# Four graph layers on one core: message sums of the first layer into fixed PSUM regions, PE's targets loaded once a slot

## The reference

```python
# layer 0 (the one that the change is in)
msg  = relu(x[src] + edge_attr @ We + be)
aggr = segment_sum(msg, dst, num_segments=N)
h    = x + aggr
h    = relu(h @ W1 + b1) @ W2 + b2            # then batch norm and relu
# layer 1: two graph convolutions with weights d(u)^-1/2 d(v)^-1/2
# layer 2: two relation layers
agg   = segment_sum(transformed[etype, src] * (1 / in_degree[dst]), dst)
h_new = agg + h @ loop_w[l] + bias[l]
# layer 3: ten steps  out = spmm(out) * 0.9 + h * 0.1
```

## Time and profile before

| | us |
|---|---|
| median of 3 runs | 9681.38 |
| lowest, highest | 9676.89, 9699.11 |
| the profiled execution, its own time | 9793.55 |
| its span, first to last instruction | 9791.8 |

### The profile page before, as it was taken

One profiled execution on the slowest core, in us unless ns is written; L12 is line 12 of the kernel. 1 busy time (PEld: TensorE's weight loads), 2 busy tenths in 40 slices (PEclk: granted clock), 3 DMA queues, 4 the chain that ended last, 5 costly groups with the idle time before them and its releaser, 6 DMA issues.

```text
span 9791.8 us, 148708 instructions
## 1 busy us (share of the span) xinstructions
PE 5881.1 (60%) x46808; PEld 4498.4 (46%) x46879; DVE 2645.2 (27%) x5985; ACT 1603.6 (16%) x3420; POOL 3344.2 (34%) x3295
## 2 busy tenths in 40 slices
PE   4444433576766666788533333532323499999998
PEld 3222221222222222288332323332323399999998
DVE  4000000344444444322422222322222411111112
ACT  1111111011233344200211111111111000000000
POOL 1444455433333333100166566266565300000000
PEclk7555555555555555599756656755655599999999
DMA  5111113411222222144222222422222366666665
GB/s 219 41 41 40 38 44 56 50 42 48 53 53 58 58 62 62 18 161 161 92 63 64 55 63 57 112 56 58 59 63 56 79 198 199 198 199 199 198 200 168
DMA packets 531551, 915.44 MB, mean 93 GB/s; under 512 B 223435, under 2 KB 365788, under 8 KB 530220
## 3 DMA queue, kind: packets, MB, share of 16 engines
q1 hardware_dynamic: 285688, 621.27, 20.7%
q0 software_dynamic: 104896, 162.89, 8.2%
q10 hardware_dynamic: 140646, 128.06, 4.2%
HBM read 705.38 MB, written 205.67 MB: 93 GB/s over the span
## 4 chain that ended last, share of the span: by engine, by line
PE 51%; issue 19%; another core or an unknown queue 18%; DVE 6%; ACT 3%; DMA 2%; DVEq 1%; ACTq 1%; POOL 0%; SPq 0%; POOLq 0%
PE bank L1311 24%; PE bank L1194 9%; PE bank L1178 5%; PE bank L1265 4%; PE bank L1047 2%; DMA relation_table<-staged_records 1%; PE bank L1336 1%; PE bank L1329 1%; DVE edge_sums L1723 1%; PE bank L1109 1%; PE bank L1112 1%; ACT staged_records L808 1%; PE bank L1097 1%; DVE onehot L1642 1%
## 5 line engine op out<-in xcount | busy, mean ns | idle before, releaser
L709 POOL DMA_INDIRECT rows<-relation_table,staged_rows x1664 | 1687.6, 1014 | 2035.1 <-DMA staged_rows<-table_rows_of_tiles 1545.1
L1194 PE MATMUL bank<-staged_records 128*128 128x448 f16 x2304 | 1066.3, 566 | 634.8 <-issue 588.3
L1311 PE MATMUL bank<-own_term,h_transposed 128*128 128x192 f16 x16464 | 1378.3, 247 | 105.7 <-DVE own_term L1838 98.0
L1311 PEld LDWEIGHTS bank<-own_term,h_transposed 128*128 128x128 fp8e4 x16464 | 1364.9, 98 | 107.2 <-issue 106.4
L709 POOL DMA_INDIRECT rows<-node_table,records_in x832 | 897.2, 1078 | 1411.3 <-DMA records_in<-rec_dst 1128.5
L694 POOL DMA_INDIRECT rec_dst<-staged_records,staged_record_rows x781 | 753.3, 965 | 919.0 <-ACT staged_record_rows L817 536.3
L1311 PE MATMUL bank<-own_term,staged_records 128*128 128x192 f16 x12348 | 1032.4, 246 | 0.0
L1311 PEld LDWEIGHTS bank<-own_term,staged_records 128*128 128x128 fp8e4 x12348 | 1020.0, 98 | 0.0
L1723 DVE TENSOR_TENSOR edge_sums<-edge_sums,bank 128x96 f32 x1664 | 421.3, 253 | 1989.8 <-PE bank L1265 1474.0
L1194 PEld LDWEIGHTS bank<-staged_records 128*128 128x128 f16 x2304 | 239.9, 104 | 1417.6 <-issue 1389.8
L1675 DVE TENSOR_SCALAR staged_records<-column_numbers,table_rows_of_tiles,source_column 128x896 f16<-128x896 f16 x1152 | 602.7, 523 | 722.8 <-PE bank L1194 587.9
(11 more groups left out here) (300 smaller groups left out, 4997.3 us busy)
## 6 DMA issues: line engine op xcount, KB each, us to landing
h_transposed<-edge_counts SPq DMA_DIRECT2D x280, 784.0 KB, 4.2
staged_records<-edge_counts SPq DMA_DIRECT2D x210, 784.0 KB, 4.2
h_transposed<-edge_counts_T SPq DMA_DIRECT2D x56, 784.0 KB, 4.2
rec_dst<-records_in SPq DMA_DIRECT2D x80, 520.0 KB, 8.6
records_in<-rec_dst SPq DMA_DIRECT2D x104, 400.0 KB
edge_counts_T<-staged_records ACTq DMA_DIRECT2D x343, 112.0 KB
staged_records<-edge_counts_T ACTq DMA_DIRECT2D x49, 784.0 KB
edge_counts<-staged_records ACTq DMA_DIRECT2D x49, 784.0 KB
```

The lines of the kernel that those rows point to most:

```text
L709: pool.indirect_dma_start(out=rows[:, g, j, 0:D], out_offset=None, in_=source, in_offset=at(ap=index(g, j), axis=0)).then_inc(gathered[g], 16)
L1194: last = nc.tensor.matmul(psum[:, bass.ds(at + j * BANK, HALF)], place_oh[i], code_oh[i][:, j * HALF:(j + 1) * HALF], start=False, stop=Tr ...
L1311: last = nc.tensor.matmul(banks[j][:, 0:2 * D], slots[c][:, at:at + P], z[:, c * SB + i, :], start=(c == 0 and i == 0), stop=(c == SG - 1 ...
```

## The change

- `message_sums`: tile j of a slot goes to the fixed region `message_sum(j)` (banks 4 and 5, four tiles each), which each matmul starts afresh. PE loads no address for it.
- `pair_targets`: ahead of a slot's messages PE loads the addresses of all 12 pairs and 6 cell numbers. `pair_sums` waits for the one-hots and for the cell once for two pairs, with the cell of the second.
- `keep_sums` becomes `add_sums`: DVE loads the slot's 8 block numbers and adds all 8 regions to `acc_and_n` (97 columns a block, the count beside the sums), each add waiting for the one before it. No branch, no clearing of regions. `sums_kept` now counts tiles.
- The tables `tile_bank` and `tile_at` go; `acc_and_n` is cleared ahead of the loop, and of the PSUM only banks 0 to 3.
- After the loop the counts are copied to `deg["dst"]`; `sum_edges` no longer clears `acc`, its callers do, earlier.
- The relation tables are staged in six buffers, not two; the four new ones lie in the room of `rows`.

```diff
         xs = sb("x_residual", [P, W])
         h = sb("h", [P, W])
-        acc = sb("edge_sums", [P, W])
+        acc_and_n = sb("edge_sums", [P, NB * RS])
+        acc = acc_and_n[:, 0:W]
...
-        rel_st = stage_flat[:, 0:2 * RELS * D].rearrange("p (s w) -> p s w", s=2)
+        REL = 6
+        rel_st = [stage_flat[:, i * RELS * D:(i + 1) * RELS * D] for i in range(2)] \
+            + [flat[:, i * RELS * D:(i + 1) * RELS * D] for i in range(REL - 2)]
...
+        def message_sum(j):
+            return banks[4 + j // 4][:, (j % 4) * RS:(j % 4 + 1) * RS]
...
                     sp.wait_ge(rel_b, r + 1)
-                    sp.dma_start(table_rel_rows[:, b, :], rel_st[:, r % 2, :]).then_inc(rel_out[r % 2], 16)
+                    sp.dma_start(table_rel_rows[:, b, :], rel_st[r % REL]).then_inc(rel_out[r % REL], 16)
...
             def message_sums(g, G):
-                at = values_of(pe, tile_bank, G * GT, 1, 4 * BANK, 6 * BANK)[0]
                 pe.wait_ge(onehot_ready, G + 1)
                 pe.wait_ge(msg_ready, G + 1)
                 for j in range(GT):
-                    nc.tensor.matmul(psum[:, bass.ds(at, RS)], onehot[:, g % 2, j * P:(j + 1) * P], rows[:, g, j, :],
-                                     start=False, stop=True, skip_group_check=True).then_inc(rows_free, 1)
-                    if j + 1 < GT:
-                        at = values_of(pe, tile_bank, G * GT + (j + 1), 1, 4 * BANK, 6 * BANK)[0]
-
-            def pair_target(k):
-                return (values_of(pe, pair_q, k, 1, 1, CELLS + 1)[0], values_of(pe, pair_at, k, 1, 0, 2 * BANK)[0])
-
-            def pair_sums(k0):
-                q, at = pair_target(k0)
+                    nc.tensor.matmul(message_sum(j), onehot[:, g % 2, j * P:(j + 1) * P], rows[:, g, j, :],
+                                     start=True, stop=True).then_inc(rows_free, 1)
+
+            def pair_targets(G):
+                return (values_of(pe, pair_q, G * PAIR_RING, PAIR_RING, 1, CELLS + 1),
+                        values_of(pe, pair_at, G * (2 * PAIR_RING), 2 * PAIR_RING, 0, 2 * BANK))
+
+            def pair_sums(k0, q, at):
                 for k in range(2 * PAIR_RING):
                     i = k % PAIR_RING
-                    pe.wait_ge(pair_ready, k0 + k + 1)
-                    pe.wait_ge(cells_free, q)
-                    pe.sem_inc(begun, 1)
+                    if k % 2 == 0:
+                        pe.wait_ge(pair_ready, k0 + k + 2)
+                        pe.wait_ge(cells_free, q[k // 2])
+                        pe.sem_inc(begun, 1)
                     for j in range(2):
-                        last = nc.tensor.matmul(psum[:, bass.ds(at + j * BANK, HALF)], place_oh[i],
+                        last = nc.tensor.matmul(psum[:, bass.ds(at[k] + j * BANK, HALF)], place_oh[i],
                                                 code_oh[i][:, j * HALF:(j + 1) * HALF], start=False, stop=True,
                                                 skip_group_check=True)
                     last.then_inc(pairs_done, 1)
-                    if k + 1 < 2 * PAIR_RING:
-                        q, at = pair_target(k0 + (k + 1))
...
                     for g in range(SLOTS):
+                        q, at = pair_targets((it + at_round) * SLOTS + g)
                         message_sums(g, (it + (LAG + at_round)) * SLOTS + g)
-                        pair_sums((it + at_round) * (SLOTS * 2 * PAIR_RING) + g * (2 * PAIR_RING))
+                        pair_sums((it + at_round) * (SLOTS * 2 * PAIR_RING) + g * (2 * PAIR_RING), q, at)
...
-            then(V.memset(psum[:, 0:6 * BANK], 0.0))
+            then(V.memset(psum[:, 0:4 * BANK], 0.0))
+            then(V.memset(acc_and_n[:, :], 0.0))
+            dve.sem_inc(sums_kept, 1)
...
-            def keep_sums(G):
-                of, after = blocks_of(dve, tiles_dst, G * GT)
-                of = of + after
+            def add_sums(G):
+                of = values_of(dve, tiles_dst, G * GT + PADT, GT, 0, NB - 1)
                 dve.wait_ge(rows_free, G * GT + (GT + SLOTS * GT))
-                dve.sem_inc(begun, 1)
                 for j in range(GT):
-                    with dve.If(of[j + 1] != of[j + 2]):
-                        at = values_of(dve, tile_bank, G * GT + j, 1, 4 * BANK, 6 * BANK)[0]
-                        V.tensor_copy(deg["dst"][:, bass.ds(of[j + 1], 1)], psum[:, bass.ds(at + D, 1)])
-                        V.tensor_copy(acc[:, bass.ds(of[j + 1] * D, D)], psum[:, bass.ds(at, D)]).then_inc(sums_kept, 1)
-                        b = limits_of(dve, tiles_dst, G * GT + (j + PADT), 1, 0, NB - 1)[0]
-                        dve.wait_ge(sums_kept, b + 1)
-                        dve.sem_inc(begun, 1)
-                        V.tensor_copy(psum[:, bass.ds(at, RS)], no_sum[:, :])
+                    dve.wait_ge(sums_kept, G * GT + (j + 1))
+                    a = acc_and_n[:, bass.ds(of[j] * RS, RS)]
+                    V.tensor_tensor(a, a, message_sum(j), ALU.add).then_inc(sums_kept, 1)
```

More of the change, by code:

```diff
@@ L455, in build @@
         rel_b = sem("rel_b")
-        rel_out = [sem(f"rel_out{j}") for j in range(2)]
+        rel_out = [sem(f"rel_out{j}") for j in range(REL)]
         t_ps = sem("t_ps")
@@ L728, in gather_relations @@
             def gather_relations(l, first):
-                for j in range(2):
-                    pool.wait_ge(rel_out[j], 16 * (((l + 1) * NB + 1 - j) // 2))
+                for j in range(REL):
+                    pool.wait_ge(rel_out[j], 16 * (((l + 1) * NB + REL - 1 - j) // REL))
                 gather_all(table_rel, first)
@@ L893, in _ @@
             keep_cells(NB - 1, 0)
-            act.wait_ge(sums_kept, NB)
+            act.wait_ge(sums_kept, T + 1)
             act.wait_ge(pairs_done, PAIRS + PAIR_RING)
@@ L1703, in _ @@
                         records_read(G)
-                        keep_sums(G)
+                        add_sums(G)
                 at_round, lo = at_round + rounds, hi
@@ L1707, in _ @@
             dve.wait_ge(cells_free, CELLS + 2)
-            dve.wait_ge(sums_kept, NB)
+            dve.wait_ge(sums_kept, T + 1)
+            then(V.tensor_copy(deg["dst"][:, :], acc_and_n[:, :].rearrange("p (b w) -> p b w", w=RS)[:, :, D]))
             def sum_edges(first, places_of):
-                then(V.memset(acc[:, :], 0.0))
                 def slot_onehot(it, g):
@@ L1738, in sum_edges @@
                 add_slot(ROUNDS - 1, SLOTS - 1)
-            V.tensor_tensor(h[:, :], h[:, :], acc[:, :], ALU.add).then_inc(hT_in, 1)
+            V.tensor_tensor(blocks(h), blocks(h), acc_and_n[:, :].rearrange("p (b w) -> p b w", w=RS)[:, :, 0:D],
+                            ALU.add).then_inc(hT_in, 1)
             then(V.tensor_reduce(most[:, :], over[:, :], X, ALU.max))
@@ L1806, in relation_layer @@
                 dve.sem_inc(hT_in, 1)
+                then(V.memset(acc[:, :], 0.0))
                 projected(2 + l, tab, None, bias2[:, l, :])
```

31 lines of the change are left out of this document (12 added, 19 removed).

## The result

The changed kernel takes 9250.0 us (median of 4 runs, 9214.2 to 9256.1) where the kernel before takes 9689.8 beside it: ratio 0.9539 [0.9511, 0.9567], 440 us less. Timed again, with five runs, it took 9247.2 against 9690.0: 0.9537 [0.9518, 0.9556]. The forecast was 9175, its range 9050 to 9340.

The account below looks back on a forecast made before the run. The prediction took PE's sequencer, with its register loads, to bound the edge loop. Savings of 481 us (loop) and 28 (tables), less 3 before the loop, made 506 off the 9681.4 median: 9175 us, range 9050 to 9340.

Parts of the forecast that it names:

- DVE's chain: First layer's edge loop: DVE's one-hots, head and sums take 16.05 us a slot and are the next bound.
- Short cells: Last half of the edge loop: slots take 0.5 to 1 us more, put at 0.4 on the mean.
- The loads: PE at the slot's head: two loads, 0.52 + 0.76 = 1.3 us a slot, covered by array work or waits for DVE.
- PE's slot of 13.4 with 4 us of slack: Edge loop after the change: PE needs 3.4 + 9.0 + about 1 us, inside DVE's 17.7.
- PE's slot as a sum of messages and pairs: Edge loop before: pairs 17.5, messages 5.0 and idle 0.6 us add up to the 23.1 us slot.
- rival D: PE's pair gaps come from computed addresses and waits, so pairs stay at 1.46 us: 9502 us; chance 0.03.
- Rival A: PE's clock rises in the edge loop: 16.8 us a slot, saving 605, time 9050 us; chance 0.15.
- Rival B: In short cells PE, waiting for two pairs and ACT, empties DVE's ring: 200 us back, 9375 us; chance 0.18.
- Rivals C: Slower: DVE's chained adds for all 832 tiles cost 1.1 us each, slot 23.8 us, time 9723 us; chance 0.03.
- Tables: Relation tables: six staging buffers remove waits for the DMA, saving 14 us a layer, 28 in all.
- Before the loop: Ahead of the edge loop: clearing acc and counts costs 4.0 us, clearing less PSUM saves 0.9: +3 us.
- the 112 between profile and median: Whole kernel before: median 9681.4 us lies 112 below the profiled execution; the same 506 was subtracted from the median.

Follow-up runs that it names:

- experiment 9: Kernel of experiment 7 with two rounds in each turn of DVE's pair loop, on group A: 9181.2 us, 0.9479 of the kernel before.
- experiment 7: Changed kernel with the pair targets loaded behind the message matmuls, run three times on group B: 8095.9, 8084.1 and 8103.5 us.
- Experiment 6: Changed kernel with only every second message sum added by DVE, on group A: 9202.6 us against the changed kernel's 9247.2.
- Experiment 3: Changed kernel with pair targets loaded pair by pair again and two staging buffers, on group B: 8212.6 us, 0.948 of the kernel before.
- experiment 4: Kernel before with PE's eight message address loads made one load ahead of the messages, on group A: 9426.7 us against 9690.0.
- 2: Kernel before with pair targets loaded once a slot and one wait for two pairs, on group B: 8327.4 us, 0.9606 of the kernel before.
- 8: Kernel of experiment 7 with waits pair by pair again and twelve cell numbers loaded, on group B: 8143.0 us, 0.9412 of the kernel before.
- group A: Runs on chip 8, where the kernel before takes 9690 us.
- group B: Runs on chips 7, 4 and 3, where the kernel before takes 8657 to 8662 us; the changed kernel itself was not timed there.
- experiment 1: Kernel before with six staging buffers for the relation tables instead of two, on group B: 8639.5 us against 8660.3.
- Experiment 5: Kernel before with all PE targets loaded once a slot and waits by two pairs, DVE's branches kept, on group B: 8204.2 us against 8656.7.

## Why the prediction was right, and where it was not

**The loop: right to 2 us by its sum (1738 forecast, 1740 and 1764 measured), by terms that erred both ways.** DVE's chain was put at 16.05 us; the floor is 16.02. "3 us of going back to the top" is 4.4 (20.38 less 16.02), 0.35 a slot more. The 0.9 a slot of issue stalls carried over from the earlier trace rows are about 0.3 in the first quarter, 0.6 less. Short cells were put at 0.4 on the mean; the first two quarters run at 17.4 a slot, the third at 18.7, the last at 19.0, which is 0.7 on the mean. These errors cancel.

**The loads, "1.3 us a slot", hidden: mis-sized, and hidden only in part.** I priced a further value at 0.04 us from the earlier trace rows, which are 32-bit values; that gave 0.76 for twelve (measured 0.86) and 0.52 for six (measured 1.46, since these are 16-bit). The loads stand ahead of the messages and not beside the array's work; experiment 9 leaves 0.1 to 0.3 us a slot for that, experiment 7, across the groups, 0.6 or more.

**PE's slot of 13.4 with 4 us of slack: too short.** Experiment 6 takes 1.5 us a slot from DVE, and the slot falls by 0.6 in the first quarter and not at all in the last two.

**PE's slot as a sum of messages and pairs: good for the kernel before, wrong as a price for each part.** 17.5 + 5.0 + 0.6 gives its 23.1 us. By the same sum fixed regions alone would bring 1.6 us a slot, 154 us (rival D). Experiment 3 brought 429 us in the loop (2193 to 1764), since the sequencer runs ahead of the array as soon as the messages need no load. The forecast of the whole change was spared this error, as it was bounded by DVE's chain.

**Rival A's premise came true, its price did not.** The granted clock rose from 0.50 to 0.72; a matmul of 448 columns takes 432 ns instead of 566. PE's busy share of the loop fell meanwhile from 69% to 56%; what grew is the length of the runs without a gap. The clock follows the loads that are gone: 0.59 in experiment 4, 0.64 in 3, 0.67 in 2, 0.74 in 7. In the changed kernel a run of products without a gap that begins at 2689.7 us has 0.50 granted up to 2694 and 1.00 from 2696 to 2702, and is back at 0.50 after a pause of 4.4 us in PE's work (from 2704). The risen clock bought little in the early slots, as PE waits for DVE there. With the rule I had named from the Trainium skill, "TensorE: Matmul & The Clock Gate", Part 1, that activity releases the throttle, the trace agrees in this; the 9050 us did not follow from it.

**Rival B is there as a tail.** ACT is hardly waited for more (27 and 42 us in the two profiles, in place of 32); slots of the last quarter are 1.6 us longer than the first's, not 3.4 (the terms written there add up to 21.7, not 21.9). Rivals C and D are out: eight chained adds are 3.06 us, and the gaps went with the loads (experiments 2 and 8).

**Tables: 28 forecast, 31 measured.** PE's pitch of 1.3 a block was met exactly (1.29). **Before the loop: +3 forecast.** In group A the first message product comes 8 and 13 us earlier than before, the first pair 11 and 19, more than the bounds given. But experiment 4, which changes nothing ahead of the first message product, has them 12 and 13 us earlier too, so most of that is not the change's. In group B, against experiment 1, the kernels with the new tables have the first message product within 1.2 us and the first pair 4 to 6 us earlier.

**The term that cost 75 us: the 112 between profile and median.** The forecast for a profiled execution, 9287, was 73 too high for the first (9214) and about 30 for the second (span 9255.5). Then I took the same 506 off the median of before, so that the forecast of the timed runs came out 75 too low. The changed kernel has no such gap between profile and median: its first profiled execution is 36 under its median, its second some 10 over. What is visible of the excess of before lies in untouched stages: the relation edge loops took 1371 and 1375 us in its profile, and 1332 to 1370 and 1340 to 1350 in the five other profiles of group A. Against the middle of these that is some 50 of the 104 to 112 us; where the rest was stays open. Timed, the change takes 440 to 443 us, against the sum of 506.

## What to carry to other kernels

Count an engine's sequencer as a resource of its own: a register load between two matmuls does not add its time to a gap only, it stops the sequencer from running ahead, and taking a few away can bring more than the loads' own time (experiment 4: 263 us, where eight loads of 0.30 us became one of 0.60, an estimated 173 us by themselves). Two edits on the same queue don't add (333 and 448 us alone, 440 to 443 together with the tables): price each with the other done. Put a bulk load right behind a batch of instructions that needs none, not ahead of it, and look at the width of the values. Compare two versions on one chip: here the changed kernel never ran beside experiments 5 and 7, and that leaves the worth of the regions and of the move open.

## What the runs showed of the hardware

A load of several registers took longer for the table of 16-bit values than for the tables of 32-bit ones. Twelve of 32 bits took 0.86 us, eight 0.60, one 0.31, so 0.05 for each further one; six of 16 bits 1.46, twelve 2.86, so 0.23. The Trainium skill, "Runtime: NRT & Kernel Launch", section "Instruction fetch mechanics", gives about 200 ns a register even in bulk, for registers that the runtime has loaded from HBM. The loads here read a table in SBUF: the 16-bit ones come near that figure, the 32-bit ones are four times quicker.

With DVE's branches gone the program fetches fewer instructions. A row of the page's DMA queues (packets, MB, share), of the kernel before:

```profile
q14 instruction: 249, 2.04, 0.1%
```

And of the changed kernel:

```profile
q14 instruction: 171, 1.40, 0.1%
```

The same row has 249 in experiments 1, 2, 4 and 5, which keep the branches, and 171 in 3, 7 and 8, which don't. (167 in 6, 147 in 9.) Experiment 5, in which PE hardly loads, still has DVE's stalls before the one-hot, 246 us; experiment 3, in which PE loads pair by pair and DVE has no branches, has 62. So they belong to the branches and not to anything on PE. Experiment 3's wait:

```profile
DVE onehot L1639 <- issue: 61.5, 21, 3.3
```

Chips of the same kind differed by 1000 us on the same kernel, nearly all of it in stages ahead of the changed loop and in the relation layers; what makes it was not looked into. In group A POOL waits 526 us for ACT's staging in the first stage, in group B 0.3 us (experiments 1 and 7). The waits of the changed kernel, 200 to 1700 us:

```profile
POOL rec_dst L698 <- ACT staged_record_rows L821: 525.9, 16, 58.9
```
